# The row normalisation of layer 1's attention: from VectorE to ScalarE, with a shift from GpSimd

## What is computed

```python
def _layernorm(x, axis=-1, eps=1e-05):
    m = jnp.mean(x, axis=axis, keepdims=True)
    v = jnp.var(x, axis=axis, keepdims=True)
    return (x - m) / jnp.sqrt(v + eps)
...
x = x + _L0_xattn_ref(_layernorm(x, axis=-1), ctx, ctx, Wq, Wk, Wv, Wp)
x = x + _L0_ffn_ref(_layernorm(x, axis=-1), router_w, w1, w2)      # 8 experts, the best 2 per row
x = x + _L1_xattn_ref(ctx, ctx, _layernorm(x, axis=-1), Wv, Wk, Wq, Wo, bo)
x = x + _L1_ffn_ref(_layernorm(x, axis=-1), U1, V1, b1, U2, V2, b2)
```

## Time and profile before

| what | value |
|---|---|
| median of 3 runs | 1107.93 us (1105.76 to 1111.91) |
| the profiled execution | 1103.02 us, span 1101.2 us |
| attention of layer 1 within the span | about 769 to 989.5 us |
| busy over the whole span | PE 83%, DVE 58%, ACT 45%, POOL 38% |
| mean granted clock of PE | 0.921 |

### The profile page before, as it was taken

The page is one execution under the profiler, slowest core; times in us unless marked ns, Lnnn a source line. Parts: engine busy times, 40 slices in busy tenths (PEclk is TensorE's granted clock), DMA queues, the critical chain, the costliest instruction groups (busy, mean ns, idle before and its releaser), DMA issues. The chain is left out here.

```text
span 1101.2 us, 24348 instructions
## 1 busy us (share of the span) xinstructions
PE 918.6 (83%) x8038; PEld 630.3 (57%) x8038; DVE 640.5 (58%) x1554; ACT 490.3 (45%) x832; POOL 417.8 (38%) x560
## 2 busy tenths in 40 slices
PE   6789999997412999999999999997378888877996
PEld 4445555553202888889888988875124444443552
DVE  4556777774697444545444444443698888435561
ACT  1487777775222333333333333322055555634653
POOL 2476776761100334242312222110875553004440
PEclk9799999998655999999999999999589999996998
DMA  6332434331523111111112121111632221000122
GB/s 178 65 105 61 118 97 122 94 105 61 176 83 115 35 54 45 54 47 51 53 45 58 40 58 40 49 31 32 172 92 73 71 66 34 1 1 1 47 51 58
DMA packets 76289, 75.45 MB, mean 69 GB/s; under 512 B 25290, under 2 KB 69434, under 8 KB 76186
## 3 DMA queue, kind: packets, MB, share of 16 engines
q1 hardware_dynamic: 69706, 56.31, 17.6%
q0 software_dynamic: 6480, 17.70, 6.1%
HBM read 51.64 MB, written 22.34 MB: 67 GB/s over the span
## 5 line engine op out<-in xcount | busy, mean ns | idle before, releaser
L1327 DVE CAST hh_e<-h_e 128x512 f16<-128x512 f32 (+1 forms) x156 | 66.7, 427 | 213.2 <-ACT h_e L1303 123.4
L1253 PE MATMUL up_ps<-xT_e,experts 128*128 128x256 f16 (+1 forms) x624 | 165.1, 266 | 4.8 <-ACT h_e L1303 3.2
L1255 PE MATMUL up_ps<-xT_e,experts 128*128 128x256 f16 (+1 forms) x624 | 165.1, 265 | 0.0
L1254 PE MATMUL up_ps<-xT_e,experts 128*128 128x256 f16 (+1 forms) x624 | 164.3, 264 | 0.0
L1267 PE MATMUL y_ps<-experts,hh_e 128*128 x568 | 155.1, 273 | 1.2 <-DVE hh_e L1329 0.3
L1268 PE MATMUL y_ps<-experts,hh_e 128*128 x568 | 155.1, 273 | 0.0
L1269 PE MATMUL y_ps<-experts,hh_e 128*128 x568 | 154.9, 273 | 0.0
L1188 POOL COPY idx_e<-token 128x2 int32 (+2 forms) x39 | 22.5, 577 | 304.6 <-PE xT_ps_e L1233 249.6
L1303 ACT ACTIVATE h_e<-up_ps 128x512 f32<-128x512 f32 (+1 forms) x156 | 87.2, 559 | 109.1 <-PE up_ps L1255 109.1
L1329 DVE TENSOR_TENSOR hh_e<-h_e,hh_e 128x512 f16<-128x512 f32 (+1 forms) x156 | 100.6, 645 | 5.4
L1537 ACT ACTIVATE prob_a<-sT_ps_a 77x1024 f32<-77x1024 f32 x64 | 64.8, 1014 | 50.4 <-PE sT_ps_a L1467 50.4
(11 more groups left out here) (275 smaller groups left out, 1938.0 us busy)
## 6 DMA issues: line engine op xcount, KB each, us to landing
experts<-in_L_ffn_w SPq DMA_DIRECT2D x22, 512.0 KB, 4.1
y_scratch<-y_e SPq DMA_DIRECT2D x32, 256.0 KB, 3.0
w_r<-in_L_ffn_w SPq DMA_DIRECT2D x10, 512.0 KB, 3.8
x<-in_x SPq DMA_DIRECT2D x32, 128.0 KB, 4.1
experts<-in_x SPq DMA_DIRECT2D x64, 64.0 KB, 2.4
x_scratch<-experts SPq DMA_DIRECT2D x16, 256.0 KB, 2.5
xh_scratch<-experts SPq DMA_DIRECT2D x16, 256.0 KB, 2.7
x_a<-x_scratch SPq DMA_DIRECT2D x32, 128.0 KB, 2.1
```

What stands on the lines that cost most here:

```text
L1253: mm(out, w[0], xT[0][:, c, 0:W_], start=c == 0, stop=False)
L1254: mm(out, w[0], xT[1][:, c, 0:W_], start=False, stop=False)
L1255: last = mm(out, w[1], xT[0][:, c, 0:W_], start=False, stop=c == DC - 1)
L1327: nc.vector.tensor_copy(hh[0][own], h[own]).then_inc(hhi_ok, 1)
```

## The change

VectorE no longer normalises rows in `attend`. ScalarE does, as Identity(rstd * X + shift), with shift = -mean * rstd from a new instruction of GpSimd behind the pow, which waits for the pow's semaphore. ScalarE's order within a step now begins with `normed_rows(f + 1)`, ahead of `exps(k, 0)`; it waits for shift_ok, and for the transposes of two tiles before. PE and the bias on GpSimd wait for xh_ok as before. The first parts of the diff, which add the tile shift_a and the semaphore shift_ok, are left out.

```diff
@@ -1417,6 +1417,9 @@
                     pool.wait_ge(var_ok, f + 1)
                     nc.gpsimd.tensor_tensor(rstd[:, f % 4, :], ve[:, f % 4, :], G["neghalf"][:, :], ALU.pow) \
                         .then_inc(rstd_ok, 1)
+                    pool.wait_ge(rstd_ok, f + 1)
+                    nc.gpsimd.tensor_scalar(shift[:, f % 4, :], mv[:, f % 4, 0:1], rstd[:, f % 4, :], -1.0, ALU.mult, ALU.mult) \
+                        .then_inc(shift_ok, 1)
                     if f > 0:
                         biased(f - 1)
                 biased(NT - 1)
@@ -1531,6 +1534,12 @@
                     nc.scalar.activation(xhi[:, f // 4 % 3, :, flat(f % 4, P)],
                                          t_ps.rearrange("p (c t) -> p c t", c=DC), ACT.Copy).then_inc(hi_ok, 1)
 
+                def normed_rows(f):
+                    act.wait_ge(shift_ok, f + 1)
+                    after(act, t_done, f - 1)
+                    nc.scalar.activation(xh[:, f % 2, :], X[:, f, :], ACT.Identity, bias=shift[:, f % 4, :],
+                                         scale=rstd[:, f % 4, :]).then_inc(xh_ok, 1)
+
                 def exps(k, half):
                     act.wait_ge(sT_done, 2 * k + half + 1)
                     after(act, v_done, k - 1)
@@ -1554,6 +1563,8 @@
 
                 for k in STEPS:
                     f, n = k + 5, k - 5
+                    if tile(f + 1):
+                        normed_rows(f + 1)
                     if 0 <= k < QUARTERS:
                         exps(k, 0)
                     if tile(n):
@@ -1588,12 +1599,6 @@
                     dve.wait_ge(ch, 2 * f + 2)
                     nc.vector.tensor_scalar(ve[:, i, :], mv[:, i, 1:2], EPS, None, ALU.add).then_inc(var_ok, 1)
 
-                def normed_rows(f):
-                    dve.wait_ge(rstd_ok, f + 1)
-                    after(dve, t_done, f - 1)
-                    nc.vector.tensor_scalar(xh[:, f % 2, :], X[:, f, :], mv[:, f % 4, 0:1], rstd[:, f % 4, :],
-                                            ALU.subtract, ALU.mult).then_inc(xh_ok, 1)
-
                 def low(f):
                     dve.wait_ge(hi_ok, f + 1)
                     place = (slice(None), f // 4 % 3, slice(None), flat(f % 4, P))
@@ -1637,8 +1642,6 @@
                         heads(n)
                     if tile(f):
                         maximum(f, 0)
-                    if tile(f + 1):
-                        normed_rows(f + 1)
                     if tile(f + 2):
                         rows(f + 2)
                     if tile(n):
```

More of the change, by code:

```diff
@@ L1350, in attend @@
         stats, mv = L.sb("stats_a", [P, 4, 6]), L.sb("mv_a", [P, 4, 2])
-        ve, rstd = L.sb("ve_a", [P, 4, 1]), L.sb("rstd_a", [P, 4, 1])
+        ve, rstd, shift = (L.sb(f"{n}_a", [P, 4, 1]) for n in ("ve", "rstd", "shift"))
         xh = L.sb("xh_a", [P, 2, D])
@@ L1369, in attend @@
         y_in = [L.sem(f"y_in{i}_a") for i in range(4)]
-        bo_in, xb_ok, xa_ok, x2_ok, ch, var_ok, rstd_ok, xh_ok = (
-            L.sem(f"{n}_a") for n in ("bo_in", "xb_ok", "xa_ok", "x2_ok", "ch", "var_ok", "rstd_ok", "xh_ok"))
+        bo_in, xb_ok, xa_ok, x2_ok, ch, var_ok, rstd_ok, shift_ok, xh_ok = (
+            L.sem(f"{n}_a") for n in ("bo_in", "xb_ok", "xa_ok", "x2_ok", "ch", "var_ok", "rstd_ok", "shift_ok", "xh_ok"))
         t_done, hi_ok, lo_ok, s_done, max_ok, mc_ok, mT_done, mT_ok = (
```

## The result

The changed kernel has a median of 1112.68 us, the kernel before, run beside it on the same chip, 1109.1 us. The ratio is 1.0033 with an interval of 1.0017 to 1.0050: slower by 3.7 us (1.9 to 5.5), and within the 0.5% (5.5 us) that the prediction took as no change. One of the 22 executions of the changed kernel, at 4822 us, is a slow one and not in the ratio. The profiled execution took 1113.25 us (span 1111.4) against 1103.02 before. Single executions of the kernel before lie anywhere from 1102 to 1114 us, over all chips that it ran on, so one profiled execution of each doesn't give the difference; the stage has to be measured by itself.

The account below looks back on a forecast made before the run. Full steps were taken as bound by a ring of PE's 4.0 us plus about 1.5 us of handovers. First exps 0.75 us late plus 0.05 for rounding gave +0.8 us: 1103.8 profiled, 1108.7 median, range 1103.5 to 1113.5.

Parts of the forecast that it names:

- the likeliest case: Whole kernel: the forecast together with no effect, -0.2 to +1.8 us including a one-time slow start; chance 0.65.
- Part 1: DVE loses 32 normalising instructions of 0.405 us, 13 us in all; nothing comes off the 20 full steps.
- Part 2: POOL gains the shift behind its own wait: 0.30 us a tile, a turn of 4.0 us while the pipeline fills.
- The rival of a shift as dear as the pow: POOL's shift costs 0.65 us a tile in place of 0.30, giving 1111.2 us; chance 0.13.
- Part 3: ACT normalises at the head of a step for 0.55 us (0.38 to 0.64), hidden in its idle time before exps.
- Part 4: At the first exps, the table load waits behind tile 6's normalisation, so exps start 0.75 us late.
- The rival of the clock: PE's granted clock is still low in step 1, doubling 1.5 us of its work: 1110.2 us; chance 0.05.
- the ring of 4.31 us: Steps 0 to 4: a loop of ACT and PE work, 4.31 us a turn, carries the first exps' delay on.
- The gain of the filling: While the pipeline fills, DVE's lost work saves 7 x 0.4 = 2.8 us, giving 1105.1 us; chance 0.07.
- Identity runs between exps without one: Rival judged: Identity isn't in Exp's table, so each step has two loads, 43 us over 27 steps: 1151; chance 0.03.
- the change has no effect: Rival: the load is placed ahead of ACT's rows, time 1107.9 us; shares the forecast's chance of 0.65.

Follow-up runs that it names:

- e5: The changed kernel again, unaltered, for a second profile; ratio 1.0028 against the kernel before.
- e4: The changed kernel with ACT's normalisation of the next tile placed behind the first exps of a step instead of ahead; ratio 1.0111 against the kernel before.
- e3: The changed kernel without POOL's shift: ACT normalises with the mean as bias (wrong values, same durations), waiting for the pow alone; ratio 0.9994 against the kernel before.
- e2: The changed kernel with DVE normalising again, while POOL still makes the shift, which nobody reads; ratio 1.0022 against the kernel before.
- e1: The changed kernel with a one-column Exp ahead of ACT's steps, so the table loads early; ratio 0.9983 against the kernel before.
- e9: The changed kernel with five unused matmuls at the end of PE's step 0; ratio 0.9996 against the kernel before.
- e7: The changed kernel with a one-column Copy, which needs no table load, ahead of ACT's steps; ratio 1.0044 against the kernel before.
- e10: e8 with twelve unused matmuls added on PE in steps -4 to 0; ratio 0.9967 against the kernel before.
- e11: The kernel before with twelve unused matmuls added on PE in steps -4 to 0; ratio 0.9973 against the kernel before.
- e8: e1 with the shift moved from POOL to ACT, made from a one-column -mean that DVE writes; ratio 0.9981 against the kernel before.
- e6: The kernel before again, unaltered, for a second profile; ratio 1.0009 against the kernel before.

## Why the prediction was right, and where it was not

The number held: 1112.7 against 1108.7, inside 1103.5 to 1113.5, and the difference is within 0.5%. Much of that is the width of the range, and of the 4.0 us between the two medians 1.2 are the kernel before itself, which ran at 1109.1 and not at the 1107.93 that the forecast started from. The forecast difference was +0.8 us and the measured one is +3.7, beyond the upper end of the likeliest case (+1.8): the time was right in part by luck, and two terms of the sum were not.

**Part 1 holds.** Results 0 to 19 take 109.81 us in before and in e5 and 109.79 to 109.83 in all the others but e4 and after's one execution. DVE now waits about 0.5 us in each of the steps for the projection.

**Part 2, the shift's price, is the first term that was mis-sized.** Forecast were 0.30 us a tile and a turn of 4.0 us; measured are 0.49 to 0.52 and 4.23. In the rows of POOL above, the shift starts 0.69 us after the pow and the bias 0.34 us after the shift, 1.03 in all; in e3, without the shift, the bias starts 0.54 us after the pow. Of these 0.49 us, 0.15 is the wait for the pow's own semaphore, for which I had put 0.08 since I hadn't seen that without it the bias starts before the pow's end. The other 0.34 is the shift, forecast at 0.22: it takes 0.265 us in the full steps and 0.38 where DVE's two additions run beside it, and the second of them, beside the shift's end and the bias, takes 1.06 us in place of 0.485. In e2 the bias (0.97 in place of 0.72) and that addition (0.83) are both longer. So POOL and DVE slow each other down, and DVE is as full in these turns of 4.23 us as POOL. The Trainium skill, "GPSIMD Engine Reference", Specifications, says that GpSimd shares its SBUF interfaces with VectorE, with contention where a DVE instruction has two SBUF inputs; these durations agree, since the additions have two such inputs. The rival of a shift as dear as the pow wasn't the case either, but the truth lies between it and the forecast.

**Part 3 holds in substance.** The rows cost ACT 0.598 us, forecast 0.55 and at most 0.64, and are hidden at the head of a step. e4 shows what they cost where they aren't: 0.42 us a step.

**Part 4 had the mechanism and not the size.** The load stands behind the rows of tile 6 and exps behind the load, as forecast. It was to make the first exps 0.75 us late; they are 1.9 (e5) to 2.1 us (after) late, since the six turns of POOL before it and the tile's own pow and shift each took 0.2 us more than forecast. Loaded early (e1), 0.7 us of that remain. The rule of the Trainium skill ("ScalarE: Activation LUTs", What ACT_TABLE_LOAD costs) that puts about 1380 ns of drain beside a load would have given +2.1 us. That is the number that came out, but for another reason, and this trace doesn't agree with the rule: the load starts 0.02 us behind the rows (807.08 + 0.60, then 807.70) and exps start 0.01 us behind the load, so there is no room for a drain.

**The rival of the clock came true, beside the forecast and not in its place.** I gave it 0.05 and 1.5 us, for PE's work of step 1 alone. In e5 it is 2.3 us, because the low level lasts until 816 us, through step 2. The step that failed is the assumption in the sum that the ring of 4.31 us carries the delay on unchanged. The prediction itself said that PE would wait 1 us longer just behind a rise of the clock; it should have had more than one chance in twenty. e9 shows that this part is the clock's, and e1 beside e7 that it hangs on the load. The clock fell in step 1 in all three traces with the load behind the rows and nothing added on PE (after, e5, e7), and not in e9's one trace, where PE was kept busy.

Together: 1.9 + 2.3 = 4.2 us in the stage of e5, and 1.0028 to 1.0033 or 3 to 4 us in the timed runs.

**The other rivals fell.** The gain of the filling exists, but is smaller than the 2.8 us that I priced and needs POOL free and the clock up: in e3, without the shift, exps come 1.45 us sooner, and the shift, with the load that it delays, takes that away and 2 us more. With both conditions met (e10 against e11) the stage is 2.5 us shorter. Only one table load is in the stage; and Identity runs between exps without one. That the change has no effect is out by the interval.

## What to carry to other kernels

An instruction that is put ahead of the first use of a table in an engine's queue also goes ahead of the load: see whether the load had been in idle time, and if so load the table early with an activation of one column. Price a small instruction on an engine that sets the pace by start-to-start distances, and beside what its neighbours then do, not by its own length; here the short one on POOL cost 2 us (e2), and on ACT, where there was idle time, 0.2 (first exps of e8 against e3). Where PE comes out of a half-idle stretch, look whether its granted clock is up before counting a gain or a delay in front of it: in these runs it was worth 1.7 to 7.8 us, where the rest of the change cost 1.9 to 2.1. A few unused matmuls held it in e9 and e10; in e11 it fell again in spite of them.

## What the runs showed that was not expected

PE's granted clock fell from its 2.4 to its 1.2 GHz level in step 1 in after, e5 and e7, behind idle times of 2.41, 2.42 and 2.86 us, and didn't with 1.24, 1.25 and 1.42 us (e6, e1, e9). In e8 it fell once more without a long one, in e4 it didn't rise before 820 us and in e3 not before 828. What the low level cost from the first exps to result 0 was 1.7 us in e7, 2.3 in e5, 3.6 in e8, 4.7 in after and 7.8 in e3, beyond the 23.65; each is one execution. Which of its conditions decides wasn't settled.

A DVE addition of 128x256 with two inputs took 1.06 us beside POOL's shift and bias, and 0.485 alone; in e2 it took 0.83 and the bias beside it 0.97 in place of 0.72.
